# GpSimd takes the last product of each expert pair in the third and fourth layer of a four-layer network

## The reference, cut to what matters

```
u = x @ w1[e]          # 512 tokens x 64
v = x @ w3[e]
y += (gate[:, e] * silu(u) * v) @ w2[e]
```

## Time and profile before

| what | value |
|---|---|
| time, median of 3 runs | 4112.48 us (4109.26 to 4114.49) |
| profiled execution | 4112.52 us |
| its span | 4110.7 us |
| PE busy | 3090.2 us, 75% |
| DVE busy | 2462.4 us, 60% |
| ACT busy | 1673.9 us, 41% |
| POOL busy | 678.4 us, 17% |
| L1250 on POOL, 320 of them | 429.5 us |
| L1480 on DVE, 336 of them | 229.0 us |
| L1485 on DVE, 336 of them | 249.3 us |

### The profile page before, as it was taken

How to read it: one execution, slowest core, us unless ns; L and a number is a source line. 1 busy time by engine, 2 the same in 40 slices (tenths; PEclk the granted TensorE clock), 3 DMA queues, 4 the chain that set the end, 5 groups by cost and what they waited for, 6 DMA issues and landing times.

```text
span 4110.7 us, 43879 instructions
## 1 busy us (share of the span) xinstructions
PE 3090.2 (75%) x16174; PEld 1576.0 (38%) x16174; DVE 2462.4 (60%) x4568; ACT 1673.9 (41%) x2458; POOL 678.4 (17%) x465
## 2 busy tenths in 40 slices
PE   4468758886698758896588857987489965897588
PEld 1124323543245423553235422453235532355145
DVE  5535866478555775558654775558755586533542
ACT  3315514454344524455144543445244551442141
POOL 2001201311022101312013010221013120121020
PEclk7569879997999889998899979998899988998696
DMA  2430183303741064301832036411643018321251
GB/s 87 51 106 1 41 137 104 96 0 80 117 136 45 23 95 134 112 14 42 138 116 83 1 89 111 140 38 27 103 129 107 13 42 138 120 76 38 59 179 53
DMA packets 332143, 330.82 MB, mean 80 GB/s; under 512 B 101449, under 2 KB 267145, under 8 KB 331657
## 3 DMA queue, kind: packets, MB, share of 16 engines
q1 hardware_dynamic: 331928, 328.01, 34.0%
HBM read 278.88 MB, written 47.78 MB: 79 GB/s over the span
## 4 chain that ended last, share of the span: by engine, by line
PE 52%; DVE 28%; DMA 5%; ACT 5%; SPq 5%; issue 4%; POOL 1%; ACTq 0%; DVEq 0%; POOLq 0%
DVE MX L1438 6%; PE PS L1638 6%; PE PS L1658 6%; PE PS L1662 5%; PE PS L1494 5%; DVE U L768 5%; PE PS L1502 5%; PE PS L950 3%; PE PS L1607 3%; DVE U L761 2%; DMA D<-e_scratch 2%; DVE XN L450 2%; PE PS L1618 1%; ACT D L1305 1%; SPq L598 1%
## 5 line engine op out<-in xcount | busy, mean ns | idle before, releaser
L1250 POOL TENSOR_TENSOR D<-D,GW 128x512 f32<-128x512 f32 x320 | 429.5, 1343 | 1486.6 <-ACT D L1324 1255.1
L654 ACT ACTIVATE U<-U 128x2048 f32<-128x2048 f32 x256 | 488.6, 1908 | 214.2 <-DVE U L768 141.5
L1480 DVE SCALAR_TENSOR_TENSOR D<-D,PS 128x512 f32<-128x512 f32 x336 | 229.0, 682 | 429.6 <-ACT D L1327 344.1
L1324 ACT ACTIVATE D<-PS 128x512 f32<-128x512 f32 x336 | 200.2, 596 | 591.7 <-PE PS L1658 591.4
L1662 PE MATMUL PS<-XT,WST 128*128 128x512 f32 (+1 forms) x672 | 367.7, 629 | 78.0 <-DVE D L1480 78.0
L1638 PE MATMUL PS<-WST,D 128*128 128x128 f32 (+1 forms) x2688 | 387.1, 289 | 44.6 <-DVE D L1485 43.9
L1638 PEld LDWEIGHTS PS<-WST,D 128*128 128x128 f32 (+1 forms) x2688 | 353.6, 200 | 172.3 <-DVE D L1485 102.0
L768 DVE SCALAR_TENSOR_TENSOR U<-PP,RD,QB 128x512 f32<-128x512 f32 x512 | 367.1, 780 | 29.7 <-ACT QB L651 29.0
L950 PE MATMUL PS<-U,resident 128*32 128x512 f32 x2048 | 312.2, 688 | 92.3 <-ACT U L654 91.9
L1438 DVE TENSOR_REDUCE MX<-PS 128x2 f32<-128x1024 f32 x256 | 292.8, 1218 | 141.0 <-PE PS L1585 141.0
L1658 PE MATMUL PS<-XT,WST 128*128 128x512 f32 (+1 forms) x672 | 371.7, 636 | 6.1 <-DMA WST<-in_pairs_dram 5.3
(11 more groups left out here) (350 smaller groups left out, 4094.3 us busy)
## 6 DMA issues: line engine op xcount, KB each, us to landing
GW<-gates_scratch SPq DMA_DIRECT2D x320, 256.0 KB, 4.2
WST<-in_pairs_dram SPq DMA_DIRECT2D x336, 192.0 KB, 2.3
U<-band_scratch SPq DMA_DIRECT2D x32, 1280.0 KB, 14.5
UU<-in_w_dram SPq DMA_DIRECT2D x64, 512.0 KB, 7.0
UU<-q_scratch SPq DMA_DIRECT2D x24, 384.0 KB
UU<-k_scratch SPq DMA_DIRECT2D x24, 384.0 KB
e_scratch<-D SPq DMA_DIRECT2D x8, 1024.0 KB, 6.0
D<-e_scratch SPq DMA_DIRECT2D x32, 256.0 KB, 11.2
```

The source lines that it names most:

```text
L654: e.activation(ring(i), ring(i), ACT.Gelu).then_inc(S["act"], 1)
L1250: e.tensor_tensor(AV[:, n % 3, :], AV[:, n % 3, :], GW[:, p // 2 % GWS, p % 2, :], ALU.mult).then_inc(S["gated"], 1)
```

## The change

The last product of a pair moves from DVE to POOL. In `b_pool_pairs` POOL now has, for each pair, the product with the gate, and behind it AV = AV x SL, which waits for its own product with the gate and for DVE's `uv`. The next pair's product with the gate stands behind that on POOL. For the shared pair POOL has the last product only. The corresponding instruction is gone from `b_dve_pairs`:

```diff
         def b_pool_pairs(e, b, l):
-            for p in range(npair(l)):
-                yield pair_at(l, p) + 2
-                n = first(l) + p
-                e.wait_ge(S["sl"], at("sl", b, 2 * n + 1))
-                if p % 2 == 0:
-                    e.wait_ge(S[f"gw_in{p // 2 % GWS}"], at(f"gw_in{p // 2 % GWS}", b, 32 * (p // 2 // GWS) + (32 if l == 2 else 64)))
-                e.tensor_tensor(AV[:, n % 3, :], AV[:, n % 3, :], GW[:, p // 2 % GWS, p % 2, :], ALU.mult).then_inc(S["gated"], 1)
+            for p in range(npair(l) + 1):
+                n, m = first(l) + p, P if p < npair(l) else 64
+                if p < npair(l):
+                    yield pair_at(l, p) + 2
+                    e.wait_ge(S["sl"], at("sl", b, 2 * n + 1))
+                    if p % 2 == 0:
+                        e.wait_ge(S[f"gw_in{p // 2 % GWS}"], at(f"gw_in{p // 2 % GWS}", b, 32 * (p // 2 // GWS) + (32 if l == 2 else 64)))
+                    e.tensor_tensor(AV[:, n % 3, :], AV[:, n % 3, :], GW[:, p // 2 % GWS, p % 2, :], ALU.mult).then_inc(S["gated"], 1)
+                yield pair_at(l, p) + 3.4
+                if p < npair(l):
+                    e.wait_ge(S["gated"], at("gated", b, p + 1 + (0 if l == 2 else E2 // 2)))
+                e.wait_ge(S["uv"], at("uv", b, n + 1))
+                e.tensor_tensor(AV[0:m, n % 3, :], AV[0:m, n % 3, :], SL[0:m, n % 3, :], ALU.mult).then_inc(S["av"], 1)
...
         def b_dve_pairs(e, b, l):
...
                 e.scalar_tensor_tensor(out=SL[0:m, n % 3, :], in0=SL[0:m, n % 3, :], scalar=1.0, in1=PZ(1)[0:m, :], op0=ALU.add, op1=ALU.mult).then_inc(S["uv"], 1)
-                yield pair_at(l, p) + 3.4
-                e.wait_ge(S["uv"], at("uv", b, n + 1))
-                if p < npair(l):
-                    e.wait_ge(S["gated"], at("gated", b, p + 1 + (0 if l == 2 else E2 // 2)))
-                e.tensor_tensor(AV[0:m, n % 3, :], AV[0:m, n % 3, :], SL[0:m, n % 3, :], ALU.mult).then_inc(S["av"], 1)
```

```diff
         def thread(part, e, turn):
             for b in range(B):
-                for t in part(e, b):
+                t = 0.0
+                for x in part(e, b):
+                    t = t if x is None else x
                     yield (b + turn) * TURN + t
...
             yield 389.5
             e.wait_ge(S["b_f"], at("b_f", b, 3))
-            e.activation(XN(b), GB(b), ACT.Tanh).then_inc(S["b_t"], 1)
+            e.activation(SB(b), GB(b), ACT.Tanh).then_inc(S["b_t"], 1)
```

More of the change, by code:

```diff
@@ L366, in weave @@
             ahead = [[next(p, None), k, p] for k, p in enumerate(programs)]
-            ahead = [x for x in ahead if x[0] is not None]
             while ahead:
@@ L520, in a_norm_act @@
             yield t + 5
+            if l == 0 and b >= 2:
+                e.wait_ge(S["v2_ps"], at("v2_ps", b - 2, PAIRS))
             e.wait_ge(S["a_xt_ps"], at("a_xt_ps", b, l + 1))
@@ L529, in a_sp @@
                 e.wait_ge(S["x_saved"], at("x_saved", b - 2, 16))
+                e.wait_ge(S["b_xn"], at("b_xn", b - 2, 2))
             e.dma_start(X(b), a["x"][b].rearrange("(j p) c -> p j c", p=P)).then_inc(S["x_in"], 16)
@@ L639, in a_act @@
                     for h in range(2):
+                        yield
+                        if b >= 2:
+                            e.wait_ge(S["b_x"], at("b_x", b - 2, 3))
                         e.wait_ge(S["l0_ps"], at("l0_ps", b, 6 + h))
@@ L810, in a_dve @@
             e.wait_ge(S["f0_ps"], at("f0_ps", b, 4))
+            if b >= 2:
+                e.wait_ge(S["g_saved"], at("g_saved", b - 2, 16))
             e.tensor_tensor(GB(b), tiles(PS(3)), XN(b), ALU.add).then_inc(S["a_f"], 1)
@@ L1206, in b_sp @@
                 gate_load(e, b, 3, q)
[L1207 to L1211, removed]
+            for x in range(E1):
+                yield 283 + 0.6 * x
+                if x == 0:
+                    e.wait_ge(S["pv3"], at("pv3", b, 16))
+                    if b == B - 1:
+                        sp_before_final(e)
+                if b + 1 < B:
                     w1_load(e, b + 1, x)
-            else:
-                e.wait_ge(S["pv3"], at("pv3", b, 16))
-                sp_before_final(e)
             for p in range(PAIRS3):
@@ L1260, in b_act @@
                     yield f1_at(x) + 1.1 + 2.1 * f
+                    if b > 0 and x == 0 and f == 0:
+                        e.wait_ge(S["n_saved"], at("n_saved", b - 1, 32))
                     e.wait_ge(S["h1_ps"], at("h1_ps", b, NF * x + f + 1))
@@ L1451, in b_dve @@
             e.wait_ge(S["b_t"], at("b_t", b, 3))
-            e.scalar_tensor_tensor(out=GB(b), in0=XN(b), scalar=1.0, in1=GB(b), op0=ALU.add, op1=ALU.mult).then_inc(S["b_x"], 1)
+            e.scalar_tensor_tensor(out=GB(b), in0=SB(b), scalar=1.0, in1=GB(b), op0=ALU.add, op1=ALU.mult).then_inc(S["b_x"], 1)
         def dve_sum(e, b, n):
```

30 lines of the change are left out of this document (23 added, 7 removed).

## The result

The changed kernel takes **4164.41 us** (median; 4162.17 to 4170.37) against 4110.87 for the kernel before beside it: ratio **1.0132, 95% interval 1.0114 to 1.0149**. It is slower, and by 53 us instead of the 11 forecast; the range ended at 4146.

The account below looks back on a forecast made before the run. No single engine was taken as the bound: two threads share engines in fixed order, the chain changing between PE and DVE. 21.0 - 11.2 + 0.9 = +10.7 on 4112.52 gave 4123 us, range 4098 to 4146.

Parts of the forecast that it names:

- Rival 1: POOL's product slips in ahead of the long addition; third layer gains about 1 us a round, total 4095; chance 0.23.
- Rival 2: Slack catches one of two long-addition patterns; third layer costs 1.6 a round, as much as fourth brings: 4113; chance 0.15.
- TensorE's clock ... so I count 0: At third-layer `down` products, two slow-clock pauses get shorter and two new ones come up: 0, at worst +3 a round.
- Rival 3: Same order as forecast, but both new third-layer pauses drop PE to 1.2 GHz: +3 a round, 4144; chance 0.14.
- +3.0 a round forecast: Third layer beside A's bonds: both threads leave the stage some 3 us late; seven rounds +21.0, bounds -6.2 and +9.
- about four more POOL products fall into groups of L768 (+4.1): Third layer: four more POOL products in a stage fall into DVE's groups of four additions, costing DVE 4.1 us.
- The row's 1.02 a product: Third layer: each POOL product inside four L768 additions costs DVE 1.02 us, from 2.73 undisturbed and 4.76 with two.
- -1.6 a round forecast: Fourth layer beside A's attention: its parts sum to -1.6 us a round, seven rounds -11.2, bounds -11 and +3 a round.
- the -0.6 of the first part: Fourth layer, first part: DVE's 3.35 us reciprocal starts without L1485 ahead and POOL serves the next `down`: -0.6 us.
- The late pairs: Fourth layer, last part: one `down` 1.9 us earlier, of which 1.0 is left at the next pair; -1.0 in all.
- The last round: B runs alone: +0.8 for free pairs, twice +0.6 at layer ends, -0.4 at third layer's start, -0.7 at reciprocal: +0.9.
- rival 4: POOL bounds every free pair: 0.15 us instead of 0.03 on some 15 pairs in eight rounds, +14, 4137; chance 0.08.

Follow-up runs that it names:

- e13: The whole change plus nine extra matmuls a round in TensorE's pauses behind the third layer, against the kernel before: 4158.78 us, ratio 1.0111.
- e12: Kernel before with only the fourth layer's last products moved to POOL, in all rounds but the last: 4111.56 us, ratio 0.9997.
- e14: Kernel before with last products of third-layer pairs 0 and 1, fourth-layer pairs 25 to 31 and shared expert on POOL, rounds 1 to 7: ratio 1.0023.

## Why the prediction was wrong

**The sign, the place and the pattern were right.** POOL's last products of pairs 2 and 6 last 3.18 and 3.20 beside a long addition, `down` waits for them, and the order on DVE is the one forecast: L770 straight behind L1512. Rival 1 (POOL slips in) is refuted by the same rows. Rival 2 (one of the two patterns is caught by slack) is half right: pair 2 on top of pair 6 costs nothing (87.33 against 87.26), but only where no other product is moved.

**The step that failed most is "TensorE's clock ... so I count 0".** It looked for the clock at the `down` products of pairs 2 and 6. There it cost little: 1.66 and 1.16 instead of 1.05 to 1.16. The clock was lost one stage further, in a pause that both kernels have, since it came back later: +2.5 us a round, 17.6 in all, shown by e13 (all of it gone with the pause filled) and by the 0.50 against 1.00 in every round. This holds for the first result; the repeat on another chip has the slow query matmuls in four rounds of seven, so how large this term is differs by the set. Rival 3 had a price of this size (+3 a round) at the wrong place, and its test would have called it false.

**The third layer was mis-sized**: +3.0 a round forecast, +4.4 measured, 30.7 against 21.0 in all. By its own parts in one round: the start was right or better (`down` 1.3 and 2.2 earlier for 1.0), pair 2 late by 1.5 (1.9), pair 6 by 4.2 (3.8). The miss is behind each: pair 3 late by 3.2 (1.8), pairs 4 and 5 by 1.9 (1.1), the end by 4.7 (3). I had let "about four more POOL products fall into groups of L768 (+4.1)"; the groups grew by 44.5 us, 6.4 a round over seven. POOL works two products a pair in a row, so a group beside it can meet three and take 5.16, where the earlier trace rows has two and 4.76. Counted over the rounds, 3 POOL products begin inside such a group in the kernel before and 9 to 11 in the changed one: some seven more, not four. The row's 1.02 a product was fair (6.4 over seven is 0.9), the count was short. By the Trainium skill's rule (SBUF — State Buffer, "Who interferes with whom"), a whole 1.27 each, four products would make an estimated 5.1 and seven 8.9; the 6.4 measured lies between.

**The fourth layer did not pay**: -1.6 a round forecast; five rounds give -1.6 to +0.6, together -2.6, and the first +2.5, so -0.1 in all, and -0.5 in the seventh. In the round compared, the -0.6 of the first part did not come: `down` of pairs 6 and 7 is 0.3 late, and the full middle part takes that back to 0.0. The late pairs gained 1.95 at the first as forecast (1.9), and 0.5 at the layer's end for the 1.0. The windows say why there was so little: DVE is relieved, PE is not. The stage's three parts in the changed kernel, as in the earlier trace rows:

```profile
2128.24:2164.24 36.00, 30.62 (x149) 17.42 (x149) 26.40 (x43) 8.68 (x16) 17.73 (x15) 0.95 0.58 194
2164.24:2234.24 70.00, 66.17 (x391) 36.78 (x391) 20.20 (x36) 34.41 (x79) 44.19 (x35) 1.00 0.46 125
2234.24:2264.24 30.00, 26.30 (x111) 15.57 (x111) 13.34 (x20) 7.68 (x15) 20.73 (x16) 0.89 0.15 42
```

In the middle DVE falls from 32.8 to 20.2 of 70 us, and PE stays at 66.

**The last round** cost 1.3 + 4.4 instead of 0.9, and of this the 1.3 is not the change's for certain (above). A free pair takes 0.09 more and not 0.03: two of them 5.40 instead of 5.22 us, some 3 us over the 33 pairs, by a part of rival 4. At the end the last `down` waits 1.33 where it waited 0.72, +0.6 as forecast:

```profile
4083.90 1.26 PE L1667 MATMUL PS<-WST,D 64*128 64x128 f32 x8 [1.33 <-POOL D L1278]
```

With e12, which leaves the last round alone, this part is back at 304.86 (before 304.89). Single profiles scatter: the seven kernels that move these products have 306.83 to 309.27, mean 308.1, the other eleven 302.70 to 307.45, mean 305.1. So some 3 of the 4.4 us are the move's.

Of the 42 us between forecast and result (52.8 against 10.7) the clock is 17.6, the fourth layer 10.6, the third 9.7, the last round 4.8, and the two stages at the start -0.5.

## What to carry to other kernels

An idle engine is not free if it reads the same memory: count how many of its instructions will fall inside each long SBUF-only instruction of the other, with the new ones in a row, and look for the one that will start just before the helper is released. When a change makes a stage slip, read the granted clock in the next pause of TensorE as well, since the matmuls behind it can take twice as long in a stage in which nothing was moved (here 1.99 and 3.78). A relieved engine pays only where it, and not TensorE, ends the wait.

## What was not expected of the hardware

- After the same pause of some 7 us and the same 16 transposes at 0.50, the clock came back 5 us or more later in the changed kernel, and in e14 it did so in one round and not in the next. What decides this was not settled; the work ahead differed by 1 us.
- Holding the clock in one place (e13) returned 18 us there, and the profile was 12 longer elsewhere, for a reason that no run shows. What a local repair of the clock gives can't be read in its own stage.
- The change's price differed by the set of runs (1.0132, 1.0089), as did the time of the kernel before (4111 to 4133) and the number of rounds in which the query matmuls ran at 0.50 (seven, four).
- A DVE addition of 128x512 takes 0.68 us alone and up to 1.76 beside a POOL product of 1.27.
